# A conditioned attention block on one core: one order for the last slots, and k of tile 3, tile 4's division, tile 5's sums and x moved in the lead

## The chip, the core and the metric

The kernel runs on one NeuronCore of a Trainium2 chip. Its engines are TensorE (PE in the profile, matrix products), VectorE (DVE), ScalarE (ACT), GpSimd (POOL), and SyncE (SP), which issues most of the DMAs. They run side by side and wait for each other on semaphores only. Matrix products are written to PSUM banks (SA, SM, MB of two banks each, O and Y of one); everything else lies in SBUF. The metric is the device time of one execution in microseconds.

## What is computed

The reference, cut to what matters (16 batches of 512 tokens with 512 features; 16 heads of 32):

```
h = layernorm(x)                                   # over the features
shift, scale, gate = split(silu(time) @ mod_w + mod_b, 3)
h = h * (scale + 1) + shift
q, k, v = split_heads(h @ w_qkv)
q = rope(layernorm(q, q_norm_w), position)         # rotates the first 16 of 32 elements
k = rope(layernorm(k, k_norm_w), position)
attn = softmax(q @ k.T / sqrt(32))
out = x + (attn @ v) @ w_out * gate
```

## The kernel before, in words

Tokens are cut into 64 tiles of 128 (four a batch), heads into 64 groups of four (four a batch). Products that need precision are made in three passes, with a high part and a low part of each operand: `project` computes q, k or v of a tile with 12 matmuls of 512 columns, `project_out` the output of a tile with 12. `project_part` and `project_out(n, bank, first, last)` can run a piece of the twelve.

The order on each engine is written by hand. A lead fills the pipeline: weights are split in high and low parts, the first tiles normalized (`normalize_x`), moved, squared and summed (`square_sums`), divided by their roots (`inverse_roots`, `normalize_qk`), and rotated on GpSimd (`rotate`, three instructions for q and three for k). Then a loop of 64 slots, `for s in range(LAST + 1)`, where slot s does the attention of group s, the projections of tiles s + 4 to s + 6 and the output of tile s - 5:

- TensorE: `transpose_c(s)` (transposes the row maxima of group s), `transpose_qk(s + 1)`, then four times `scores_by_key(s, t)`, with `scores_by_query(s + 1, t)`, `weigh_values`, `add_over_keys(s - 1)`, projections and an output tile between them.
- VectorE takes the maxima of `scores_by_query` (`maxima`, two halves for each t), the low parts (`low_qk`, `x_low`), sums, roots and `apply_gate`.
- ScalarE takes the exponentials of `scores_by_key` (`key_exponentials`, two halves), and copies out of PSUM.
- GpSimd adds probs over keys: `add_keys` issues two DMAs of 1024 KB a group that add one buffer to another, `sum_keys` one addition of 2048 elements a partition; it also scales o (`scale_o`), makes its low part (`output_low`), adds the residual (`add_residual`), and rotates.

What binds them around the change: `scores_by_query(s + 1, t)` needs the first exponential of `scores_by_key(s, t)`, since both use bank SM; `scores_by_key(s, t + 1)` needs both exponentials of t and the first maximum of `scores_by_query(s + 1, t)`; `transpose_c(s + 1)` needs all eight maxima of its group. Bank Y is shared by projections, sums over keys and output tiles, one after the other.

Slots with `late(s)` (58 to 63) have no projections of q and k left. Before, slots 58 and 59 run the output tile between `scores_by_query(s + 1, 1)` and `scores_by_key(s, 2)`, slots 60 to 62 in two halves of six matmuls after the query scores of t = 0 and 1; slot 62 has one more behind its last query scores, and slot 63 one before `scores_by_key(63, 1)`. Behind the last query scores of slots 58 to 61 nothing stands.

## Time and profile before

| | |
|---|---|
| time, median of 3 runs | 1703.88 us (1703.47 to 1704.93) |
| profiled execution, own time | 1703.24 us |
| its span | 1701.0 us |
| TensorE busy | 1635.7 us (96%) |
| VectorE, ScalarE, GpSimd busy | 1238.0, 997.2, 977.0 us |
| mean granted clock | 0.987 |

The span is what the trace covers; what lies around it is 2.2 us. Times in the rows count from the start of the span. [...]

### The profile page before, as it was taken

The page shows a single profiled execution, that of the slowest core. Times are in us where ns is not written, and L with a number is a line of the kernel's source. Part 1 is how long each engine was busy: PE and PEld are TensorE (multiplying, and loading weights), DVE is VectorE, ACT ScalarE, POOL GpSimd, SP SyncE. Part 2 cuts the span into 40 slices and gives each one's busy share as a digit, 9 for nine tenths or more (in the row PEclk, how much of TensorE's full clock was granted, in tenths as well). Part 3 has the DMA queues.
Part 4 walks back from the last instruction along what each step waited for, and adds up shares of the span by engine and source line. Part 5 has one row for each costly group of instructions (what it writes and reads, how often), then busy time and mean ns, then how long its engine had stood idle before and what let it go on. Part 6 is the DMA issues. An engine that isn't in the chain of part 4 may idle for free.

```text
span 1701.0 us, 31069 instructions
## 1 busy us (share of the span) xinstructions
PE 1635.7 (96%) x11846; PEld 963.6 (57%) x11846; DVE 1238.0 (73%) x1541; ACT 997.2 (59%) x1484; POOL 977.0 (57%) x769
## 2 busy tenths in 40 slices
PE   5979999999999999999999999999999999999887
PEld 3744565556566556555656655655555665564444
DVE  8767777777777777777777777777777777776552
ACT  3445666656566566665656656666666665665552
POOL 0525556665656656666665665666666566565441
PEclk9979999999999999999999999999999999999999
DMA  6034545546455554644645555464555555545553
GB/s 218 26 69 87 122 109 134 128 106 149 112 118 131 121 134 106 151 110 111 144 112 130 119 137 118 107 149 112 125 131 119 122 120 137 116 109 117 128 112 96
DMA packets 55417, 204.25 MB, mean 120 GB/s; under 512 B 6872, under 2 KB 6872, under 8 KB 39144
## 3 DMA queue, kind: packets, MB, share of 16 engines
q0 software_dynamic: 18144, 132.13, 38.6%
q1 hardware_dynamic: 37128, 70.14, 12.8%
q8 instruction: 97, 1.59, 0.4%
q14 instruction: 48, 0.39, 0.1%
HBM read 53.25 MB, written 16.88 MB: 41 GB/s over the span
## 4 chain that ended last, share of the span: by engine, by line
PE 87%; DVE 3%; DMA 3%; issue 3%; POOL 2%; ACT 1%; SPq 0%; POOLq 0%; DVEq 0%; ACTq 0%
PE Y L339 33%; PE O L447 13%; PE SA L428 12%; PE Y L357 10%; PE SM L396 6%; PE MB L379 3%; PE SA L432 3%; PE Y L462 3%; DMA probs<-probs 2%; PE SA L331 2%; PE SA L406 1%; POOL probs L1287 1%; DMA probs<-in_L_cond_w_qkv_dram 1%; DVE cst L1053 1%; PE SM L428 0%
## 5 line engine op out<-in xcount | busy, mean ns | idle before, releaser
L1287 POOL TENSOR_TENSOR probs<-probs 128x2048 f32<-128x2048 f32 x62 | 285.5, 4605 | 334.0 <-DMA probs<-probs 334.0
L1053 DVE TENSOR_REDUCE cst<-SM 128x2 fp32r<-128x1024 f32 x256 | 313.8, 1226 | 141.1 <-PE MB L396 139.4
L808 ACT ACTIVATE probs<-SM 128x1024 f32<-128x1024 f32 x256 | 262.9, 1027 | 149.5 <-PE SM L432 140.5
L1053 DVE TENSOR_REDUCE cst<-MB 128x2 fp32r<-128x1024 f32 x256 | 311.3, 1216 | 0.0
L810 ACT ACTIVATE probs<-SA 128x1024 f32<-128x1024 f32 x256 | 260.6, 1018 | 0.0
L447 PE MATMUL O<-probs,vals 128*32 128x512 f32 x2048 | 250.8, 603 | 0.0
L339 PE MATMUL Y<-wqkv_hi,hT_lo 128*128 128x512 f32 x716 | 225.6, 411 | 0.4 <-DVE hT_lo L1037 0.4
L1260 POOL TENSOR_TENSOR pair_part<-rows,rope_pair 128x256 f32<-128x256 f32 x128 | 120.2, 939 | 171.0 <-DVE rows L1031 170.1
L339 PE MATMUL Y<-wqkv_hi,hT_hi 128*128 128x512 f32 x716 | 213.5, 420 | 0.0
L717 ACT ACTIVATE rows<-Y 128x512 f32<-128x512 f32 x121 | 72.3, 598 | 221.3 <-PE Y L339 221.3
L339 PE MATMUL Y<-wqkv_lo,hT_hi 128*128 128x512 f32 x716 | 201.5, 403 | 0.0
L1043 DVE SCALAR_TENSOR_TENSOR qk_lo<-MB,pass_w,qk_hi 128x512 fp32r<-128x512 f32 x128 | 90.7, 747 | 146.7 <-ACT qk_hi L753 146.3
L1279 POOL DMA_DIRECT2D probs<-probs x126 | 109.9, 872 | 139.0 <-PE O L447 134.1
L339 PEld LDWEIGHTS Y<-wqkv_lo,hT_hi 128*128 128x128 f32 x716 | 129.9, 188 | 75.3 <-issue 48.6
L339 PEld LDWEIGHTS Y<-wqkv_hi,hT_hi 128*128 128x128 f32 x716 | 120.6, 188 | 81.3 <-issue 23.2
L339 PEld LDWEIGHTS Y<-wqkv_hi,hT_lo 128*128 128x128 f32 x716 | 125.5, 188 | 51.1 <-issue 28.5
L396 PE MATMUL SM<-qk_hi 32*128 32x512 f32 x512 | 128.6, 498 | 15.8 <-ACT probs L808 11.0
L1066 DVE TENSOR_TENSOR gated<-Y,gate 128x512 f32<-128x512 f32 x60 | 41.5, 691 | 127.8 <-PE Y L357 127.8
L428 PE MATMUL SA<-qk_hi 32*128 32x512 f32 x512 | 128.8, 500 | 4.5 <-DVE cst L1053 3.8
L428 PE MATMUL SM<-qk_hi 32*128 32x512 f32 x512 | 129.0, 500 | 0.0
L396 PE MATMUL MB<-qk_hi 32*128 32x512 f32 x512 | 128.8, 498 | 0.0
L1293 POOL TENSOR_TENSOR oT<-oT,sum_inv 128x512 f32<-128x512 f32 x63 | 107.0, 1698 | 34.7 <-ACT sum_inv L781 34.7
(219 smaller groups left out, 3461.7 us busy)
## 6 DMA issues: line engine op xcount, KB each, us to landing
probs<-probs POOLq DMA_DIRECT2D x126, 1024.0 KB, 7.1
xin<-in_x_dram SPq DMA_DIRECT2D x62, 256.0 KB, 2.7
xres<-in_x_dram SPq DMA_DIRECT2D x60, 256.0 KB, 2.7
out_dram<-xres SPq DMA_DIRECT2D x60, 256.0 KB, 5.8
shift_scale<-mod_rows SPq DMA_DIRECT2D x15, 512.0 KB, 3.8
gate<-mod_rows SPq DMA_DIRECT2D x16, 256.0 KB, 3.3
rows<-in_L_cond_mod_w_dram SPq DMA_DIRECT2D x2, 1024.0 KB, 8.7
probs<-in_L_cond_w_qkv_dram SPq DMA_DIRECT2D x2, 1024.0 KB, 13.1
```

The costliest lines, as they stand in the source:

```text
L339: mm = pe.matmul(bank, x[:, k, :], w[:, k, cols], start=(m == 0), stop=(m == 3 * DT - 1))
L357: mm = pe.matmul(bank, o[:, g, :], w[:, g, :], start=(m == 0), stop=(m == 11))
L396: mm = pe.matmul(qm_bank(i), qk_hi[r, g % 2, 0, cols], qk_hi[r, g % 2, 1, :], start=True, stop=True)
L428: pe.matmul(s_bank(i), a[r, ring, 1, cols], c[r, ring, 0, :], start=(a is qk_hi and c is qk_hi), stop=False)
L447: mm = pe.matmul(O[head_rows(i), :], vals[:, b % 2, t, E * h:E * (h + 1)], probs[:, probs_buffer(g, t), i, :], start=(t == 0), stop=(t == ...
L808: act.activation(a[:, 2:4, :], SM[:], ACT.Exp).then_inc(s_exp, 1)
L810: act.activation(a[:, 0:2, :], SA[:], ACT.Exp).then_inc(s_exp, 1)
L1053: dve.tensor_reduce(heads[:, 2 * half:2 * half + 2, 0], (SM, MB)[half][:], AX.X, ALU.max, negate=True).then_inc(max_out, 1)
L1260: pool.tensor_tensor(pair_part[:].rearrange("p h (i two) -> p h i two", two=2), swapped, rope_pair[:, t, j, :].rearrange("p (i two) -> p i ...
L1279: pool.dma_start(probs[:, probs_buffer(g, t - 1)].rearrange("p h n -> p (h n)"), probs[:, probs_buffer(g, t)].rearrange("p h n -> p (h n)" ...
L1287: pool.tensor_tensor(total, total, part, ALU.add).then_inc(keys_summed, 1)
L1293: pool.tensor_tensor(o, o, sum_inv[:].rearrange("p (t n) -> p t n", t=TT), ALU.mult).then_inc(o_scaled, 1)
```

## The change

In the last slots, all output tiles come to stand behind the last query scores of a slot (slot 62 has a second one inside, slot 63's stands behind its third `scores_by_key`). `add_over_keys(62)` gets bank MB[1] in place of Y. `apply_gate`, `add_residual`, `output_high` and `output_low` of such a tile move to the start of the next slot. In the lead, VectorE rotates k of tile 3 (`rotate_k3`), `pass_weights` goes ahead, and on TensorE the order is another: v of tile 3 before x of tile 4 is transposed, group 0 transposed before x of tile 5, k of tile 4 cut around the first query scores, k of tile 5 in bank Y, v of tile 4 in slot 0. On VectorE, x of tile 6 goes behind the four pairs of maxima, and `square_sums(5, 0)` and `normalize_qk(4)` go into slot 0.

```diff
             def transpose_qk(g, j):
                 if i == 0:
-                    pe.wait_ge(rope_step, 6 * (TT * b + 3) + 3 * (j + 1))
+                    if b > 0:
+                        pe.wait_ge(rope_step, rope_steps(TT * b + 3, j) + 3)
+                    elif j == 0:
+                        pe.wait_ge(rope_step, rope_steps(3, 0) + 3)
+                    else:
+                        pe.wait_ge(k3_step, 3)
...
             project(2, 2, MB[:, 0, :])
-            transpose_x(4)
             pe.wait_ge(raw_out, raw_count(3, 1))
             project(3, 2, MB[:, 1, :])
+            transpose_x(4)
             modulation_parts(2, O[:])
...
@@ TensorE, the slots
-                if s > 0 and tile(s + 4):
+                if tile(s + 4):
                     if s > 1:
                         pe.wait_ge(sum_ln, s - 1)
                     if tile(s + 5):
                         pe.wait_ge(raw_out, raw_count(s + 5, 1))
+                    else:
+                        pe.wait_ge(y_gated, n)
...
-                elif group(s + 1) and n >= 0:
-                    pe.wait_ge(o_low, n + 1)
-                    pe.wait_ge(sum_ln, s - 1)
-                    project_out(n, Y[:], 0, 6)
...
                 if late(s):
                     weigh_values(s, 0)
                     if group(s + 1):
                         scores_by_query(s + 1, 1)
-                        if tile(s + 4):
-                            pe.wait_ge(o_low, n + 1)
-                            pe.wait_ge(v_out, s + 5)
-                            project_out(n, Y[:], 0, 12)
-                        else:
-                            project_out(n, Y[:], 6, 12)
...
+                    if s == LAST - 1:
+                        pe.wait_ge(o_low, n + 1)
+                        pe.wait_ge(y_gated, n)
+                        project_out(n, Y[:], 0, 12)
...
                         scores_by_query(s + 1, 3)
-                        if s == LAST - 1:
-                            pe.wait_ge(o_low, NT - TT - 1)
-                            pe.wait_ge(sum_ln, s)
-                            project_out(NT - TT - 2, Y[:], 0, 12)
+                        m = n + 1 if s == LAST - 1 else n
+                        pe.wait_ge(o_low, m + 1)
+                        pe.wait_ge(sum_ln, s)
+                        project_out(m, Y[:], 0, 12)
...
@@ VectorE
+            def rotate_k3():
+                dve.wait_ge(qk_norm, 4)
+                dve.wait_ge(silu_step, 2)
+                r = rows[:, 0, 3, 1, :].rearrange("p (h e) -> p h e", e=E)
+                part = oT_rows[:, 0, 0:H * R].rearrange("p (h r) -> p h r", r=R)
...
+                dve.tensor_tensor(part.rearrange("p h (i two) -> p h i two", two=2), swapped,
+                                  rope_pair[:, 3, 1, :].rearrange("p (i two) -> p i two", two=2)
+                                  .unsqueeze(1).to_broadcast([P, H, PAIRS, 2]), ALU.mult).then_inc(k3_step, 1)
+                dve.wait_ge(k3_step, 1)
+                dve.tensor_tensor(r[:, :, 0:R], r[:, :, 0:R], rope_same[:, 3, 1, :].unsqueeze(1)
+                                  .to_broadcast([P, H, R]), ALU.mult).then_inc(k3_step, 1)
+                dve.wait_ge(k3_step, 2)
+                dve.tensor_tensor(r[:, :, 0:R], r[:, :, 0:R], part, ALU.add).then_inc(k3_step, 1)
...
             for s in range(LAST + 1):
+                if late(s - 1):
+                    apply_gate(s - 6 if s < LAST else NT - TT - 2, Y[:], gated[:])
...
-                if s > 0 and tile(s + 5):
+                if tile(s + 5):
                     square_sums(s + 5, 0)
+                if s == 0:
+                    normalize_qk(4)
...
@@ GpSimd
                 rotate(n, 0)
-                rotate(n, 1)
+                if n != 3:
+                    rotate(n, 1)
...
+                if late(s - 1):
+                    add_residual(s - 6)
+                    output_low(s - 5)
                 if s > 0:
                     sum_keys(s - 1)
                 add_keys(s, 1)
-                if s - 5 >= 0 and not late(s):
+                if s - 5 >= 0 and not late(s) or s == LAST - 1:
                     add_residual(s - 5)
...
-                if late(s):
-                    add_residual(s - 5)
                 if s == LAST - 1:
                     output_low(s - 4)
                 add_keys(s, 3)
```

Three places in the order of the instructions. First TensorE at the end of slot 61, before: the value products of t = 2 (O), the last query scores (SM, MB), and then the transposition of the maxima (SA from cst) that opens the next slot.

```order
L447 MATMUL O<-probs,vals 32x512 x4
L396 MATMUL SM<-qk_hi 128x512 x2
L396 MATMUL MB<-qk_hi 128x512 x2
L406 MATMUL SA<-ident_r,cst 128x128 x4
L379 MATMUL MB<-ident,rows 128x128 x8
```

The same place with the change:

```order
L457 MATMUL O<-probs,vals 32x512 x4
L406 MATMUL SM<-qk_hi 128x512 x2
L406 MATMUL MB<-qk_hi 128x512 x2
L362 MATMUL Y<-wout_hi,o_hi 128x512
L362 MATMUL Y<-wout_lo,o_hi 128x512
L362 MATMUL Y<-wout_hi,o_lo 128x512
...
L416 MATMUL SA<-ident_r,cst 128x128 x4
L389 MATMUL MB<-ident,rows 128x128 x8
```

The twelve matmuls of an output tile (Y from wout and o) stand between the last query scores and the transposition.

Second, VectorE in the lead, before, from the division of tile 3 (rows from rstd) on: the low part of x of tile 4 (hT_lo), x of tile 5 (xin), the sum of the gate's parts (oT), the weights for the pass half, x_low of tile 5.

```order
L1031 TENSOR_TENSOR rows<-rows,rstd 128x1024
L1037 TENSOR_TENSOR hT_lo<-SA,hT_hi 128x512
L1021 SCALAR_TENSOR_TENSOR xin<-xin,first_stats,shift_scale 128x512
L1024 SCALAR_TENSOR_TENSOR xin<-xin,first_rstd,shift_scale 128x512
L948 TENSOR_TENSOR oT<-O,sum_inv 128x512
L1118 TENSOR_SCALAR pass_w<-pass_w 128x1
L1121 MEMSET pass_w 16x2 x4
L1037 TENSOR_TENSOR hT_lo<-SA,hT_hi 128x512
```

With the change:

```order
L1038 TENSOR_TENSOR rows<-rows,rstd 128x1024
L1061 TENSOR_TENSOR hT_lo<-SA,hT_hi 128x512
L1049 TENSOR_TENSOR oT<-rows,rope_pair 128x256
L1053 TENSOR_TENSOR rows<-rows,rope_same 128x16x16
L1056 TENSOR_TENSOR rows<-rows,oT 128x16x16
L1028 SCALAR_TENSOR_TENSOR xin<-xin,first_stats,shift_scale 128x512
L1031 SCALAR_TENSOR_TENSOR xin<-xin,first_rstd,shift_scale 128x512
L955 TENSOR_TENSOR oT<-O,sum_inv 128x512
L1067 SCALAR_TENSOR_TENSOR qk_lo<-MB,pass_w,qk_hi 128x512 x2
```

Three instructions of the rotation stand before x of tile 5, and the low parts of q and k (qk_lo) follow at once.

Third, GpSimd in slot 62, before: the sums over keys (probs), the first DMA, scale_o (oT from sum_inv), the residual, the low part of o.

```order
L1287 TENSOR_TENSOR probs<-probs 128x2048
L1279 DMA probs<-probs 128x2048
L1293 TENSOR_TENSOR oT<-oT,sum_inv 128x4x128
L1273 TENSOR_TENSOR xres<-xres,gated 128x512
L1298 TENSOR_TENSOR o_lo<-oT,o_hi 128x512
L1279 DMA probs<-probs 128x2048
```

With the change:

```order
L1299 TENSOR_TENSOR xres<-xres,gated 128x512
L1324 TENSOR_TENSOR o_lo<-oT,o_hi 128x512
L1313 TENSOR_TENSOR probs<-probs 128x2048
L1305 DMA probs<-probs 128x2048
L1299 TENSOR_TENSOR xres<-xres,gated 128x512
L1319 TENSOR_TENSOR oT<-oT,sum_inv 128x4x128
L1324 TENSOR_TENSOR o_lo<-oT,o_hi 128x512
L1305 DMA probs<-probs 128x2048
```

The residual and the low part of tile 56 and 57 open the slot, and the residual of tile 57 stands ahead of scale_o.

## Rows read from the trace of the kernel before

**Rows 1.** The page: granted clock of TensorE in 40 slices, in tenths

```profile
PEclk9979999999999999999999999999999999999999
```

**Rows 2.** Windows: stretch, length, busy of five engines, clock, DMA; slots 1, 58 to 63

```profile
122.17:146.10 23.93, 22.16 (x172) 12.26 (x171) 17.39 (x22) 14.87 (x22) 12.50 (x10) 1.00 0.48 100
1544.90:1566.54 21.64, 18.07 (x149) 9.74 (x148) 14.52 (x18) 13.79 (x20) 12.81 (x11) 1.00 0.49 99
1566.54:1590.61 24.07, 20.46 (x156) 10.95 (x157) 11.62 (x11) 12.46 (x16) 11.56 (x9) 0.93 0.55 120
1590.61:1612.12 21.51, 17.72 (x144) 8.75 (x145) 11.53 (x11) 11.97 (x15) 10.80 (x7) 0.91 0.66 141
1612.12:1634.67 22.55, 19.00 (x145) 9.24 (x145) 11.52 (x11) 12.01 (x15) 10.13 (x7) 0.86 0.55 117
1634.67:1659.69 25.02, 22.07 (x157) 11.95 (x157) 11.52 (x11) 11.74 (x15) 10.18 (x7) 0.86 0.60 127
1659.69:1701.00 41.31, 31.28 (x217) 17.47 (x215) 12.46 (x17) 11.70 (x15) 7.56 (x6) 0.95 0.31 93
```

**Rows 3.** Waits of TensorE, 1546 to 1701: us in total, times, longest

```profile
PE SA L406 <- DVE cst L1053: 9.8, 4, 2.5
PE Y L357 <- POOL o_lo L1298: 5.3, 2, 3.5
```

**Rows 4.** Timeline of slot 60: start, us, engine, line, operation, idle before and releaser

```profile
1602.40 0.50 PE L428 MATMUL SM<-qk_hi 32*128 32x512 f32 x2
...
1606.75 0.50 PE L428 MATMUL SM<-qk_hi 32*128 32x512 f32 x2
...
1609.15 0.50 PE L396 MATMUL SM<-qk_hi 32*128 32x512 f32 x2 [0.21 <-ACT probs L808]
...
1612.12 0.75 PE L406 MATMUL SA<-ident_r,cst 128*128 128x128 f32 x4 [2.46 <-DVE cst L1053]
```

**Rows 5.** Timeline of slot 58's start, and two matmuls of an output tile

```profile
1544.90 0.46 PE L406 MATMUL SA<-ident_r,cst 128*128 128x128 f32 x4
...
1546.24 0.50 PE L428 MATMUL SM<-qk_hi 32*128 32x512 f32 x2
...
1550.99 0.50 PE L428 MATMUL SM<-qk_hi 32*128 32x512 f32 x2
...
1580.09 0.39 PE L357 MATMUL Y<-wout_hi,o_hi 128*128 128x512 f32 x1
1580.32 0.39 PE L357 MATMUL Y<-wout_lo,o_hi 128*128 128x512 f32 x1
```

**Rows 6.** Timeline of slots 62 and 63: residual adds and waits for o_lo

```profile
1655.25 0.50 PE L357 MATMUL Y<-wout_hi,o_hi 128*128 128x512 f32 x1 [1.79 <-POOL o_lo L1298]
...
1664.03 1.26 POOL L1273 TENSOR_TENSOR xres<-xres,gated 128x512 f32<-128x512 f32 x1 [8.04 <-DMA xres<-in_x_dram]
...
1666.57 0.80 PE L357 MATMUL Y<-wout_hi,o_hi 128*128 128x512 f32 x1 [3.52 <-POOL o_lo L1298]
```

**Rows 7.** TensorE in the lead: a wait of 60 to 122, and the timeline

```profile
PE SM L396 <- DVE cst L1053: 4.8, 2, 4.5
...
95.62 0.72 PE L406 MATMUL SA<-ident_r,cst 128*128 128x128 f32 x4 [2.51 <-issue]
```

**Rows 8.** Timeline: GpSimd beside VectorE in slot 56, and wout_lo in the lead

```profile
1514.00 1.80 POOL L1293 TENSOR_TENSOR oT<-oT,sum_inv 128x512 f32<-128x512 f32 x1
...
1514.68 1.67 DVE L1024 SCALAR_TENSOR_TENSOR xin<-xin,rstd,shift_scale 128x512 f32<-128x512 f32 x1
...
75.00 4.58 POOL L1304 TENSOR_TENSOR wout_lo<-probs,wout_hi 128x2048 fp32r<-128x2048 f32 x1
```

**Rows 9.** VectorE's groups by form, 60 to 125: busy, mean ns, idle before

```profile
L1053 DVE TENSOR_REDUCE cst<-SM 128x2 fp32r<-128x1024 f32 x8 | 9.8, 1223 | 8.4 <-PE MB L396 8.4
L1031 DVE TENSOR_TENSOR rows<-rows,rstd 128x1024 f32<-128x1024 f32 x4 | 4.9, 1226 | 0.1
```

**Rows 10.** Windows: a stretch of slot 0, columns as in rows 2

```profile
105.00:110.00 5.00, 3.67 (x24) 1.49 (x24) 2.65 (x4) 2.98 (x5) 0.00 (x0) 0.51 0.07 25
```

More of the change, by code:

```diff
@@ L461, in add_over_keys @@
                     for i in range(HG):
-                        mm = pe.matmul(Y[head_rows(i), :], ones_r[:, 0:E].bitcast(F32),
+                        mm = pe.matmul(bank[head_rows(i), :], ones_r[:, 0:E].bitcast(F32),
                                        probs[:, probs_buffer(g, t), i, :],
@@ L528, in _ @@
             project(4, 0, Y[:])
-            transpose_x(5)
-            project(4, 1, SA[:, 0, :])
             transpose_qk(0, 0)
@@ L562, in _ @@
                         pe.wait_ge(raw_out, raw_count(s + 5, 1))
-                begun = 5 if s > 0 and not late(s - 1) else 0
+                    else:
+                        pe.wait_ge(y_gated, n)
+                begun = 5 if not late(s - 1) else 0
                 if begun:
@@ L567, in _ @@
                     scores_by_query(s + 1, 0)
-                if s > 0 and tile(s + 4):
+                if tile(s + 4):
                     project_part(s + 4, 2, Y[:], begun, 12)
-                elif group(s + 1) and n >= 0:
-                    pe.wait_ge(o_low, n + 1)
-                    pe.wait_ge(sum_ln, s - 1)
-                    project_out(n, Y[:], 0, 6)
-                if s == LAST:
-                    pe.wait_ge(o_low, NT - TT)
-                    pe.wait_ge(y_gated, NT - TT - 1)
-                    project_out(NT - TT - 1, Y[:], 0, 12)
                 scores_by_key(s, 1)
@@ L613, in _ @@
                             pe.wait_ge(v_out, s + 5)
-                        add_over_keys(s - 1)
+                        add_over_keys(s - 1, Y[:])
                 scores_by_key(s, 2)
                 if late(s):
-                    weigh_values(s, 1)
                     if group(s + 1):
+                        weigh_values(s, 1)
                         scores_by_query(s + 1, 2)
-                        pe.wait_ge(y_gated, n + 1)
-                        add_over_keys(s - 1)
-                    else:
+                        if tile(s + 4):
+                            pe.wait_ge(v_out, s + 5)
+                        pe.wait_ge(y_gated, n + 1 if s == LAST - 1 else n)
+                        add_over_keys(s - 1, Y[:])
+                    else:
+                        pe.wait_ge(o_low, NT - TT)
+                        pe.wait_ge(y_gated, NT - TT - 1)
+                        project_out(NT - TT - 1, Y[:], 0, 12)
+                        weigh_values(s, 1)
                         add_last_sums(1)
-                        pe.wait_ge(last_low, 2)
-                        project_last(0, 0, 2)
                 else:
@@ L649, in _ @@
                         pe.wait_ge(sum_ln, LAST)
+                        pe.wait_ge(last_low, 2)
+                        project_last(0, 0, 2)
+                        pe.wait_ge(y_gated, NT - TT)
                         project_last(1, 0, 2)
@@ L854, in _ @@
             move_v(2, MB[:, 0, :])
-            x_high(4)
             guess_roots(5)
             move_v(3, MB[:, 1, :])
+            x_high(4)
             move_qk(4, 0, Y[:])
-            x_high(5)
-            square(4, 0)
-            move_qk(4, 1, SA[:, 0, :])
             high_qk(0, 0)
             high_qk(0, 1)
+            square(4, 0)
             act.wait_ge(mod_product, 3)
             act.activation(mod_sb[:, 2, :], O[0:NB, :], ACT.Copy).then_inc(gate_out, 1)
+            x_high(5)
+            move_qk(4, 1, SA[:, 0, :])
             square(4, 1)
@@ L880, in _ @@
                 key_exponentials(s, 0, 0)
+                if late(s - 1) and s < LAST:
+                    output_high(s - 5)
                 key_exponentials(s, 0, 1)
@@ L887, in _ @@
                     square(s + 5, 1)
-                if s > 0 and tile(s + 4):
+                if tile(s + 4):
                     move_v(s + 4, Y[:])
@@ L912, in _ @@
                 key_exponentials(s, 3, 1)
-                if 0 <= s - 4 and s < LAST - 1:
+                if 0 <= s - 4 and not late(s):
                     output_high(s - 4)
@@ L1152, in _ @@
             first_statistics(2)
+            pass_weights()
             square_sums(2, 0)
@@ L1163, in _ @@
             x_low(4)
+            rotate_k3()
             normalize_x(5)
             modulation_sum(2, 2, O[:])
-            pass_weights()
+            low_qk(0, 0)
+            low_qk(0, 1)
             x_low(5)
@@ L1190, in _ @@
                     low_qk(s + 1, 1)
-                if s > 0 and tile(s + 5):
+                if tile(s + 5):
                     square_sums(s + 5, 0)
+                if s == 0:
+                    normalize_qk(4)
                 if group(s + 1):
@@ L1210, in _ @@
                     maximum(s + 1, 1, 1)
-                if late(s) and s < LAST:
+                if s == LAST - 1:
                     apply_gate(s - 5, Y[:], gated[:])
@@ L1330, in _ @@
                 add_keys(s, 3)
-                if 0 <= s - 4 and s < LAST - 1:
+                if 0 <= s - 4 and not late(s):
                     output_low(s - 4)
```

44 lines of the change are left out of this document (21 added, 23 removed).

## The prediction

> **What bounds the kernel now.** I read the page's clock line first. [...] TensorE is busy 1635.7 of 1701.0 us, so in the 57 slots in the middle only less matmul work would help, and the change leaves these slots as they are. It can win only where TensorE idles: in the lead (before slot 0 and in it) and in slots 58 to 63. So I read the tail slot by slot, then who TensorE waited for there, then the timeline.
>
> A slot here runs from one transposition of the row maxima (transpose_c) to the next. Slots 58 to 63 take 21.64, 24.07, 21.51, 22.55, 25.02 and 41.31 us, 156.1 in all, and from slot 59 on the granted clock is below 1 [rows 2]. The waits name two causes: 9.8 us in 4 waits for VectorE's maxima, and 5.3 us in 2 waits for GpSimd's o_lo [rows 3]. The timeline shows the first: key products start at 1602.40 and 1606.75, the last query scores at 1609.15, and then nothing until transpose_c at 1612.12, 2.46 us idle. [...] The second cause is 1.79 us idle at 1655.25 and 3.52 us at 1666.57, the latter because GpSimd had waited for a residual's load until 1664.03 [rows 6].
>
> In the lead, two waits for maxima of group 0 cost 4.8 us and one more, put down to nothing, 2.5 us; transpose_c of slot 0 starts at 95.62 [rows 7], that of slot 1 at 122.17. Slot 0 is thus 26.55 us long, against 23.93 for slot 1 [rows 2], though slot 0 has no v projection and no sums over keys.
>
> **The tail.** Nothing is removed from TensorE; the twelve matmuls of an output tile (halves of six in slots 60 and 61, a full run inside slots 58 and 59) now stand behind the last query scores. One such matmul starts 0.23 us after the other [rows 5], so the run is 12 x 0.23 = 2.75 us. It covers the 2.46 us idle: the same engine does this work while VectorE takes its two maxima. What it leaves behind is the inner intervals. An interval from key product to key product is 4.35 us [rows 4], set by a ring (exponential, query scores, first maximum), not by TensorE's work: the half runs hid inside it and it does not shrink. So the slots become:
> - transpose_c to first key product 1.34, and 4.75 us to the next where a v projection is split [rows 5]; 4.45 without filler and 5.7 where the whole run of 2.75 stands (estimates: 2.5 us until the query scores, 0.43 of them, then the maximum or the run);
> - 4.35 for each other interval; last interval 2.43 + 0.43 + 2.75 = 5.6, say 5.7;
> - slot 58: 1.34 + 4.75 + 4.35 + 4.35 + 5.7 = 20.5. Slot 59: with 5.7 in the place of 4.75, 21.4. Slots 60 and 61: with 4.45, 20.2 each.
> - Slot 62: a run in its second interval, 5.65; its last run waits for o_lo, which comes 1.26 us earlier since the residual add that stood before it moves ahead of scale_o [rows 6]. Of 1.79 us idle 0.5 stays. 1.34 + 4.45 + 5.65 + 4.35 + 6.3 = 22.1.
> - Slot 63: the run for tile 59 moves behind the third key product, where o_lo has been ready for 3 us, so the 3.52 goes. The clock of 0.95 over 41.31 us [rows 2] means 4.1 us at half clock, 2.1 of loss, which goes with the idles. In their place TensorE now waits openly for the first two exponentials: 1.0 to 1.3. 41.31 - 3.5 - 2.1 + 1.3 = 37.0, say 37.2.
>
> The sum is 141.6 against 156.1: **14.5 us less** if the clock holds. What may not hold is the clock. Seven inner intervals have now only key product, one weighing and query scores, and idle about 0.2 and 1.4 us. The nearest rows are on both sides: slot 1 idles 1.2 and 0.4 us around its second query scores and is granted 1.00 [rows 2], while every 2.46 us [rows 3] was followed by a fall. One fall costs about 1.1 us in a ring (key product 0.7, query scores 0.3). From none to five is 0 to 5.5 us. I take one, nearer to slot 1: **tail -13.3**.
>
> GpSimd's queue in a late slot becomes residual, o_lo, sum_keys, then the DMA that adds probs. The DMA of the last keys goes out about 0.25 us earlier and took some 8 us to land, so it is there 4.3 us after the next first key product; exponentials want it at 5.7. No new wait, 1.4 us to spare. SP's stores and loads of residuals start earlier relative to the end, which is what frees tile 58's.
>
> **The lead.** On VectorE k of tile 3 is three instructions of 256 elements. No row has them; a 1024-element one takes 1.23 and a 512-element one 0.69, so 0.41 each, 1.2 us, up to twice that beside GpSimd. GpSimd loses three of 0.74. So both rotations end some 2 us earlier than before, but wout_lo, one instruction of 4.58 us [rows 8], starts earlier too: at about 71.3, exactly when VectorE comes to normalize_x(5), two instructions whose inputs all lie in SBUF. [Rows 8] show what such a meeting does: scale_o, at best 1.27 us, took 1.80, since VectorE was at the first x instruction; the second x instruction then took 1.67 in place of 0.74, until GpSimd was done. Before, nothing of the kind stood beside wout_lo. So I let VectorE stand still until it ends, 75.7.
>
> [...]
>
> With the wait: x 5 is ready at 77.2, modulation_sum(2) at 77.9 (plus 0.5 since pass_weights now delays VectorE at 57), and TensorE has stood for 5 us before the gate's product. Product, copy, transposition, x_high, x_low, square sums, statistics: 5.7, to 84.1. Four pairs of maxima at 2 x 1.2 us each [rows 9], with division and square sums between and one wait for k of tile 5: 12.2, to 96.3. So transpose_c of slot 0 comes **0.7 later** than before. Slot 0 then takes what slot 1 takes, 23.93, less the 0.9 of the sums over keys, plus 0.6 of cold start: 23.6. v of tile 4, twelve matmuls, hides in intervals that idle now; the division of tile 4 delays the first maximum by 0.5, counted. Slot 1 starts at 119.9 in place of 122.17: **lead -2.2**.
>
> Sum: -13.3 - 2.2 = -15.5. The profiled execution took 1703.24 (span 1701.0 plus 2.2); the median of the runs is 1703.88, so 1703.88 - 15.5 = **1688.4 us**.
>
> **Rivals.**
> - No block in the lead. The 4.6 us instruction may give way piecemeal, or VectorE may pass before it. Then everything up to slot 1 is 4.3 us earlier: 1684. For it: no row has a block that long. Against: both meetings in [rows 8] lasted to the other's end.
> - The lean intervals lose the clock again and again: five falls in place of one, and part of the same in slot 0. 1688.4 + 4.4 + 1.5 = 1694.
> - Slower than before: the clock doesn't come back in the late slots. In slot 0 it stays at 0.51 over 105 to 110 though TensorE is busy for 3.67 of 5 us [rows 10], with gaps before the query scores and behind them, just the pattern that the change makes. If this lasts through slots 58 to 62, their 15 us of work a slot become about 28, 8 us over the interval ring's 20.2: 5 x 8 = 40 in place of a gain of 13, so 1703.9 - 2.2 - 13.3 - 1.2 + 40 = 1727. It decides from the point where two of five late slots stay at half clock throughout. Against: each slot ends in 5 us with hardly a gap, after which the rows show full clock.
> - The change does nothing in the tail, since another wait takes its place (the exponentials' wait for the DMA in slot 63, or y_gated before the sums over keys): 1701 to 1702.
>
> [...]
>
> **The numbers.** Forecast 57%, no block 22%, clock lost repeatedly 14%, no gain 3%, stuck clock 3%, 1% for the lead going wrong by itself. The range 1681.5 to 1696 takes in the first three: below it stands -6.5 in the lead with -14.5 and 1 us to spare, above it five falls and a lead that gains nothing. A difference under 0.2% (3.4 us) can hardly be told from none: faster by more 0.95, within 0.02, slower by more 0.03.
>
> **What would show it.** TensorE's waits for VectorE's maxima in the tail fall from 9.8 us to under 1, and the runs of an output tile end right before transpose_c; o_lo is waited for 0.5 us. Slots 60 and 61 are 20.2 us with clock above 0.93. In the lead normalize_x(5) shows one instruction of about 5 us beside wout_lo, and transpose_c of slot 1 stands near 119.9. I am wrong in the tail if these slots stay above 21.5 us, and in the lead if no such instruction is there.

## The result, and the profile after

The changed kernel takes **1695.78 us** (median of 6 executions, 1694.55 to 1698.43) against 1704.51 for the kernel before (6 executions, 1703.47 to 1704.93). The ratio is 0.9952, with a 95% interval of 0.9939 to 0.9965: faster by 8.2 us by the ratio and by 8.7 by the medians, where 15.5 were forecast. The time lies just inside the range, the sign is right, the size is not.

The profiled execution took 1696.27 us, its span 1694.3. This is its clock line (page of the changed kernel), the counterpart of [rows 1]:

```profile
PEclk9999999999999999999999999999999999999899
```

The dip near the start is gone from this line, and one near the end has come. The clock is a share of full clock. Over 70 to 130 us, in windows of 0.5 us, it reads 1.00 or 0.50, and something between only where it changes (0.50 from 99 to 102, 1.00 from 103 to 108): 0.50 is called the lower level, or half clock, here. To see where the time went I cut the trace at transpose_c of each slot (now L416), as in [rows 2]. Windows of the changed kernel: stretch, length, busy time of TensorE, its weight loads, VectorE, ScalarE and GpSimd, granted clock, DMA. The first row is slot 0, the others slots 58 to 63:

```profile
97.60:123.83 26.23, 24.59 (x164) 13.48 (x165) 19.66 (x25) 12.81 (x18) 10.71 (x14) 0.87 0.29 71
1546.92:1567.70 20.78, 17.99 (x149) 9.95 (x148) 14.20 (x17) 13.27 (x19) 12.70 (x11) 1.00 0.51 103
1567.70:1590.25 22.55, 20.21 (x157) 10.39 (x156) 11.53 (x11) 12.46 (x16) 10.15 (x6) 0.92 0.55 120
1590.25:1613.29 23.04, 19.71 (x145) 8.77 (x144) 11.54 (x11) 11.73 (x15) 10.06 (x6) 0.78 0.57 123
1613.29:1634.21 20.92, 17.38 (x145) 8.29 (x144) 11.53 (x11) 11.80 (x15) 9.99 (x6) 0.92 0.63 139
1634.21:1656.38 22.17, 18.83 (x157) 10.23 (x156) 12.23 (x12) 12.26 (x16) 12.53 (x8) 1.00 0.68 163
1656.38:1694.20 37.82, 29.90 (x217) 16.43 (x215) 13.41 (x17) 11.70 (x15) 7.73 (x6) 0.98 0.32 94
```

The span became 6.7 us shorter, and it splits like this:

| stretch | before | after | difference | forecast |
|---|---|---|---|---|
| start to transpose_c of slot 0 | 95.62 | 97.60 | +1.98 | +0.7 |
| slot 0 | 26.55 | 26.23 | -0.32 | -2.9 |
| slots 1 to 57 | 1422.73 | 1423.09 | +0.36 | 0 |
| slots 58 to 63 | 156.10 | 147.38 | -8.72 | -13.3 |

So the tail gives two thirds of what it should, and the lead, which should give 2.2, takes 1.7. Within the tail, slots 58 and 62 are as forecast (20.5 and 22.1). Slots 59, 60 and 61 (forecast 21.4, 20.2, 20.2) hold 4.7 us of the miss, and these three have a clock of 0.92, 0.78 and 0.92.

Waits of TensorE from 1530 to 1695 (who waited, for whom: us in all, times, longest), to be read against [rows 3]:

```profile
PE SA L438 <- DVE cst L1077: 11.0, 10, 1.4
PE SM L406 <- ACT probs L815: 3.7, 15, 0.5
...
PE Y L362 <- POOL o_lo L1324: 0.6, 1, 0.6
PE MB L472 <- DMA probs<-probs: 0.5, 1, 0.5
```

The four waits of 2.5 us ahead of transpose_c are gone and so are the long waits for o_lo, as forecast. But VectorE's maxima are still waited for, by the key products now, 11.0 us in ten pieces of up to 1.4: the idle has moved into the slots.

Timeline of slot 60, two intervals from key product to key product in which only one weighing and the query scores stand (start, us, engine, line, operation, idle before and its releaser):

```profile
1593.97 0.49 PE L406 MATMUL SM<-qk_hi 32*128 32x512 f32 x2 [0.23 <-ACT probs L815]
...
1595.89 0.50 PE L438 MATMUL SA<-qk_hi 32*128 32x512 f32 x2 [1.42 <-DVE cst L1077]
...
1597.03 1.89 PE L457 MATMUL O<-probs,vals 128*32 128x512 f32 x8
1598.85 0.79 PE L406 MATMUL SM<-qk_hi 32*128 32x512 f32 x2
...
1601.07 0.79 PE L438 MATMUL SA<-qk_hi 32*128 32x512 f32 x2 [1.43 <-DVE cst L1077]
```

After the idles of 0.23 and 1.42 us the weighing takes 1.89 us (1.07 in the interval before) and a pair of query scores 0.79 (0.49): the clock is at its lower level (0.50 from 1597.1 to 1607.4). It stays there for two intervals. In slot 58 the same two idles stand in the second interval (0.23 at 1555.43 and 1.42 at 1557.36), and the weighing behind them took 1.07 us: there the clock did not fall (1.00 over the slot). In slot 59 they stand in the second interval too (1.42 at 1579.16), and the weighing behind took 1.94: there it fell (0.50 from 1580.6 to 1582.6).

The lead: rows of all engines around wout_lo, and the two places further on where TensorE stood:

```profile
71.82 0.85 DVE L1056 TENSOR_TENSOR rows<-rows,oT 128x256 f32<-128x256 f32 x1
72.34 4.69 POOL L1330 TENSOR_TENSOR wout_lo<-probs,wout_hi 128x2048 fp32r<-128x2048 f32 x1
...
72.59 4.99 DVE L1028 SCALAR_TENSOR_TENSOR xin<-xin,first_stats,shift_scale 128x512 f32<-128x512 f32 x1
...
77.62 0.75 DVE L1031 SCALAR_TENSOR_TENSOR xin<-xin,first_rstd,shift_scale 128x512 f32<-128x512 f32 x1
...
79.03 1.89 PE L542 MATMUL O<-oT,gated 128*16 128x512 f32 x2 [5.50 <-DVE oT L955]
...
97.60 0.51 PE L416 MATMUL SA<-ident_r,cst 128*128 128x128 f32 x4 [2.51 <-issue]
```

The block is there as forecast: an instruction that takes 0.74 us without wout_lo beside it (experiment 3) lasted 4.99, until wout_lo was done (77.03), and TensorE stood for 5.50 us. No semaphore stands between the two instructions, so it isn't true of this pair that the engines wait for each other on semaphores only.

### The profile page after: what moved, and what is told of

The parts are those of the page before. It is cut to its first block, busy times and chain, and to the rows that moved or that the text cites. A ratio compares the mean times of both kernels' runs of the same rounds, so it can differ in the third digit from the quotient of the medians.

```text
span 1694.3 us, 31069 instructions
## 1 busy us (share of the span) xinstructions
PE 1633.5 (96%) x11846; PEld 959.8 (57%) x11846; DVE 1244.3 (73%) x1544; ACT 996.9 (59%) x1484; POOL 973.3 (57%) x766
## 3 DMA queue, kind: packets, MB, share of 16 engines
q0 software_dynamic: 18144, 132.13, 38.6%
q1 hardware_dynamic: 37128, 70.14, 12.9%
## 4 chain that ended last, share of the span: by engine, by line
PE 91%; DVE 4%; DMA 2%; issue 1%; ACT 1%; POOL 0%; SPq 0%; DVEq 0%; POOLq 0%; ACTq 0%
PE Y L344 33%; PE O L457 13%; PE SA L438 13%; PE Y L362 10%; PE SM L406 6%; PE SA L442 3%; PE MB L389 3%; PE Y L472 3%; PE SA L336 2%; DMA probs<-probs 1%; PE SA L416 1%; DVE cst L1077 1%; ACT probs L815 1%; DMA probs<-in_L_cond_w_qkv_dram 1%; PE SM L438 0%
## 5 line engine op out<-in xcount | busy, mean ns | idle before, releaser
L344 PEld LDWEIGHTS Y<-wqkv_lo,hT_hi 128*128 128x128 f32 x720 | 130.7, 188 | 75.5 <-issue 48.6
L1090 DVE TENSOR_TENSOR gated<-Y,gate 128x512 f32<-128x512 f32 x60 | 41.5, 692 | 128.4 <-PE Y L362 128.4
```

The source lines that it names most:

```text
L344: mm = pe.matmul(bank, x[:, k, :], w[:, k, cols], start=(m == 0), stop=(m == 3 * DT - 1))
```

## The experiments

Every kernel was timed side by side with the kernel before (1704.1 to 1704.5); times are medians, and ratios are to the kernel before beside it, with 95% intervals.

**1 and 2: the two halves of the change by themselves.** tail_only is the changed kernel with the lead, and the v projection of slot 0, as before. lead_only is the kernel before with the other part.

> Only the tail's part of the change; the lead and slot 0 are those of the kernel before. Theory A (the trace of the changed kernel is right that its lead loses 1.7 us and its slots 58 to 63 gain 8.7): the tail alone gains 8.7 us, 1704.5 - 8.7 = 1695.8, some 2 us LESS than or level with the whole change plus what its lead loses: whole change 1695.8, tail alone 1694.1. Rival B (the lead helps as predicted, and the tail gives the rest): tail alone 1698, slower than the whole change by 2. Slots 58 to 63 in the trace: 147.4 us in all, as in the changed kernel, with one to four falls of the granted clock in slots 59 to 61.

> Only the lead's part of the change; the tail is that of the kernel before. Theory A: the lead by itself costs 1.7 us, 1706.2, with transpose_c of slot 0 at 97.6 and of slot 1 at 123.8. Rival B (as predicted, the trace of the one profiled execution being untypical): it gains 2.2 us, 1702.3, with transpose_c of slot 1 near 120.

| | time | ratio | interval |
|---|---|---|---|
| tail_only | 1695.27 | 0.9946 | 0.9934 to 0.9959 |
| lead_only | 1706.06 | 1.0013 | 1.0004 to 1.0021 |

Theory A holds in the gain that it gives for the tail alone (8.7, 1695.8); its other number, 1694.1, does not come out. The tail gives 8.9 us, and the lead costs about 2 (transpose_c of slot 1 at 124.90 in lead_only). The two ratios multiplied give 0.9959, within the interval of the whole change. The whole was no slower than the tail alone by more than the measurement tells (expected 1.7, found 0.5).

**3: wout_lo later.** One wait more on GpSimd:

```diff
                     pool.wait_ge(wout_high, 1)
+                    pool.wait_ge(h_lo, 6)
                     pool.tensor_tensor(wout_lo[:], wout_raw, wout_hi[:].bitcast(F32), ALU.subtract
```

> The changed kernel, with one more wait ahead of GpSimd's wout_lo: it starts only when the low part of x of tile 5 is written (h_lo 6), so that no VectorE instruction with two SBUF inputs meets it before that. Theory A (VectorE stands still behind wout_lo for its whole 4.7 us, and this is on the path to slot 0): the first x instruction of tile 5 takes 0.8 instead of 4.99 us, the gate's product on TensorE starts near 75 instead of 79.0, and transpose_c of slot 0 near 93.5 instead of 97.6; slot 1 begins 3 to 4 us earlier, 1692 us in all. Rival C (the block is hidden: another chain, as GpSimd's q rotation or the high parts of k, would set the time anyway): transpose_c of slot 0 moves by less than 1 us and the time is that of the changed kernel.

Measured: 1688.90 us, ratio 0.9908 (0.9892 to 0.9923). Rows of late_wout: x of tile 5, wout_lo, transpose_c of slot 0, and the window of slot 0:

```profile
72.79 0.74 DVE L1028 SCALAR_TENSOR_TENSOR xin<-xin,first_stats,shift_scale 128x512 f32<-128x512 f32 x1
...
78.09 4.56 POOL L1331 TENSOR_TENSOR wout_lo<-probs,wout_hi 128x2048 fp32r<-128x2048 f32 x1 [5.51 <-DVE hT_lo L1061]
...
93.80 0.72 PE L416 MATMUL SA<-ident_r,cst 128*128 128x128 f32 x4 [2.51 <-issue]
```

```profile
93.80:121.37 27.57, 25.93 (x164) 14.79 (x165) 19.67 (x25) 13.00 (x18) 10.71 (x14) 0.82 0.28 68
```

The x instruction is back at 0.74 us, and transpose_c of slot 0 comes 3.8 us earlier. Rival C falls. The median gained 6.9, 3.1 more than that, and this trace can't show it all, since the profiled execution was the slowest of this kernel's four (1693.72; the fastest 1686.57): its slot 0 is 1.3 us longer than that of the changed kernel, at a clock of 0.82. A part it does show. Behind a wait of 1.62 us for maxima at 81.65, eight matmuls of the lead took 1.84 and 1.91 us for four (the clock is 0.50 from 83.5 to 86). In the trace of combo (experiment 6), whose lead is the same, they took 1.08 and 1.07 (1.00 from 82 to 86), and transpose_c of slot 0 came at 91.88. So the block cost 3.8 us with a fall of the clock in the lead, and 5.7 without.

**4: wout_lo in four pieces** of 512 columns, at its old place in the queue.

```diff
-                    pool.tensor_tensor(wout_lo[:], wout_raw, wout_hi[:].bitcast(F32), ALU.subtract
-                                       ).then_inc(wout_low, 1)
+                    for c in range(DT):
+                        pool.tensor_tensor(wout_lo[:, c, :], wout_raw[:, c, :], wout_hi[:, c, :].bitcast(F32),
+                                           ALU.subtract).then_inc(wout_low, 1)
```

> The changed kernel with wout_lo made by four GpSimd instructions of 512 columns in place of one of 2048, at the same place in the queue. Theory A1 (a VectorE instruction with two SBUF inputs waits for the end of the one GpSimd instruction that runs, no longer): the first x instruction of tile 5 takes at most 1.2 + 0.8 = 2 us in place of 4.99, and the second perhaps as long again; x of tile 5 is ready 2 to 3 us earlier than 78.37, and the kernel takes 1692 to 1693. Rival A2 (GpSimd keeps its hold from one instruction to the next, or the contention is by the byte and not by the instruction): the two x instructions together still take 4.5 to 5.7 us, and the time stays at 1695.8.

Measured: 1692.23 us, ratio 0.9928 (0.9916 to 0.9940). The timeline of quarters, GpSimd and VectorE:

```profile
72.42 6.03 POOL L1331 TENSOR_TENSOR wout_lo<-probs,wout_hi 128x512 fp32r<-128x512 f32 x4
...
72.66 1.76 DVE L1028 SCALAR_TENSOR_TENSOR xin<-xin,first_stats,shift_scale 128x512 f32<-128x512 f32 x1
74.45 1.64 DVE L1031 SCALAR_TENSOR_TENSOR xin<-xin,first_rstd,shift_scale 128x512 f32<-128x512 f32 x1
```

The two engines take turns: each x instruction waits for one piece and then runs, 3.4 us together in place of 5.74, and the four pieces take 6.03 in place of 4.69. So in these two traces the wait goes by the instruction that is running (Theory A1), not by the bytes: 4.99 us beside one instruction of 4.69, and 1.76 beside a piece of 512 columns, which took 1.28 to 1.71.

The same trace has a slot 0 that the others without fillers have not:

```profile
94.01:117.20 23.19, 21.53 (x165) 12.49 (x165) 19.85 (x25) 12.79 (x18) 11.39 (x14) 1.00 0.34 81
```

Its order of matmuls is that of the changed kernel, and so are its idles (2.51 us ahead of transpose_c, 1.22 and 0.41 in the second interval), yet the clock held 1.00, and the slot took 23.19 us in place of 26.23. This was one of the two fastest of six executions (1688.93; 1688.81 to 1694.89).

**5: fillers in the tail.** Matmuls whose result nobody reads, where TensorE idles 1.42 us:

```diff
+            def fill(count):
+                for _ in range(count):
+                    pe.matmul(Y[:], ident_r[:], wout_hi[:, 0, :], start=True, stop=True)
...
                     project_part(s + 4, 2, Y[:], begun, 12)
+                elif group(s + 1):
+                    pe.wait_ge(y_gated, n)
+                    fill(4)
...
                         scores_by_query(s + 1, 1)
+                        if s < LAST - 1:
+                            if tile(s + 4):
+                                pe.wait_ge(v_out, s + 5)
+                            else:
+                                pe.wait_ge(y_gated, n)
+                            fill(4)
```

> The changed kernel, with four more matmuls (128 x 512, identity times the first rows of wout_hi, into bank Y, whose content nobody reads then) behind the query scores of every lean interval: the second interval of slots 58 to 61 and the first of slots 60 to 62, 28 matmuls of 0.23 us in all. They fit into the 1.42 us that TensorE idles there. Theory D (slots 59 to 61 are 4.6 us longer than forecast because the granted clock falls in lean intervals, the ring itself being as forecast): no fall in slots 59 to 61, these slots 21.4, 20.2 and 20.2 us instead of 22.55, 23.04 and 20.92, 4 us less, 1692 in all, and the runs spread less than the 3.9 us of the changed kernel. Rival E (the slots are longer for another cause, such as VectorE, the exponentials or a DMA): no gain, and if the fillers delay the key products, 0.2 us more for each of seven intervals, 1697.

Measured: 1692.89 us (1691.19 to 1693.39), ratio 0.9933 (0.9920 to 0.9945). Windows of fill_tail, slots 59, 60 and 61:

```profile
1568.99:1590.51 21.52, 19.90 (x161) 10.88 (x160) 11.53 (x11) 12.45 (x16) 10.16 (x6) 1.00 0.57 125
1590.51:1610.61 20.10, 18.22 (x154) 9.49 (x153) 11.53 (x11) 11.86 (x15) 10.13 (x6) 1.00 0.66 141
1610.61:1630.65 20.04, 18.15 (x154) 9.47 (x153) 11.53 (x11) 11.86 (x15) 10.03 (x6) 1.00 0.66 145
```

Theory D: with eight more matmuls in slots 60 and 61 and four in slot 59, each of the three is shorter, by 1.03, 2.94 and 0.88 us, and within 0.2 of the forecast. I see nothing but the clock (1.00 now) behind it, since the fillers add work and remove no wait. Slots 58 and 62, at 1.00 already in the changed kernel, got four fillers each too and did not become shorter (20.84 and 22.23 us against 20.78 and 22.17). The median gained 2.9 and the spread fell from 3.9 to 2.2 us. The trace's gain in the three slots is 4.85; of it slot 0, which these fillers don't touch, took 1.1 back (27.36 us, clock 0.83), and slot 63 became longer (38.6 against 37.9), in it a wait of 1.1 us for the DMA that adds probs (0.5 in the changed kernel).

**6: both repairs** (late wout_lo and the tail's fillers).

> The changed kernel with both repairs: wout_lo waits for the low part of x of tile 5, and the fillers in the lean intervals. Theory: the two act at different places, 1500 us apart, so their gains add up: -6.9 (late wout_lo as measured) and -2.9 (fillers as measured) from 1695.8, 1686 us. Rival: the gains overlap, since a part of the first was luck with the granted clock in the tail; then 1689, the time of the late wout_lo alone.

Measured: 1685.49 us (1685.12 to 1690.30), ratio 0.9897 (0.9884 to 0.9909). The gains add up.

**7: fillers in the lead as well.**

```diff
             pe.wait_ge(ident_ready, 1)
+            pe.wait_ge(wout_high, 1)
+            pe.wait_ge(gate_out, 1)
+            fill_o(9)
...
                     else:
+                        if s > 0:
+                            pe.wait_ge(o_out, s)
+                        fill_o(4)
                         scores_by_query(s + 1, 1)
                         transpose_x(s + 6)
```

> The kernel with both repairs, and fillers also at the start: nine matmuls of 0.23 us into bank O while TensorE waits 2.51 us for the last maxima of group 0, and four ahead of the second query scores in slots 0 to 4, where it waits 1.23 us for exponentials. Theory F (slot 0 is 26.2 to 27.6 us long, in place of the forecast 23.6, because the granted clock is 0.5 in its first 4 us and again after the idle of its second interval): full clock throughout slot 0 and a slot 0 of 24 to 24.5 us, 3 us less than without, 1683 in all. Rival G (the ring of exponentials and maxima sets slot 0, TensorE's clock only hides in it): slot 0 changes by less than 1 us.

Measured: **1683.35 us** (1682.09 to 1683.73), ratio 0.9875 (0.9861 to 0.9889), the best of all. Windows of combo_lead, slot 0 and slot 58:

```profile
93.75:116.97 23.22, 22.72 (x168) 13.18 (x169) 19.90 (x25) 12.78 (x18) 11.41 (x14) 1.00 0.33 81
1539.91:1560.43 20.52, 19.13 (x154) 10.64 (x152) 13.82 (x17) 13.27 (x19) 12.80 (x11) 1.00 0.51 103
```

Slot 0 is 23.22 us with the clock at 1.00, against the forecast 23.6 and 26.23 to 27.57 in the traces of this lead at 0.82 to 0.87. Theory F holds. Against combo, the kernel that differs by these fillers alone, the median is 2.1 us lower; combo's profiled execution had a slot 0 of 24.58 at 0.93, and that of quarters 23.19 at 1.00, so the clock isn't lost as much in every execution.

**8: the lead's fillers alone** in the changed kernel.

> The changed kernel with the lead's fillers alone: nine matmuls of 0.23 us before transpose_c of slot 0, four ahead of the second query scores in slots 0 to 4; wout_lo stays where the change puts it. Theory F (half clock in slot 0 costs 3 us of its forecast): transpose_c of slot 0 still at 97.6 (the block stays), slot 0 23.2 us in place of 26.2, slots 58 to 63 as in the changed kernel; 1695.8 - 3 = 1692.8. Rival G: slot 0 within 1 us of 26.2.

Measured: 1692.57 us, ratio 0.9925 (0.9911 to 0.9938). Window of slot 0 of lead_fill:

```profile
97.69:120.89 23.20, 22.69 (x168) 13.21 (x169) 19.88 (x25) 12.79 (x18) 11.41 (x14) 1.00 0.33 81
```

transpose_c of slot 0 stays at 97.69, since the block is still there, and slot 0 is 3.0 us shorter. The two causes in the lead are separate: the block before slot 0, the clock in it. The tail's code is that of the changed kernel, but the falls lie elsewhere in this trace: slots 59 to 62 take 22.33, 21.02, 21.86 and 23.46 us, at 0.92, 0.92, 0.84 and 0.93.

**9: k of tile 3 rotated by GpSimd again**, in the kernel of experiment 7 (rotate_k3 taken out, `rotate(3, 1)` put back).

> The kernel with all repairs (late wout_lo, fillers in the tail and in the lead), but k of tile 3 is rotated by GpSimd again, behind q. GpSimd's three instructions of 0.74 us put the end of k at about 74.6 instead of 72.7; VectorE in turn has 2.3 us less to do and comes to x of tile 5 at 70.4 instead of 72.8. Theory K (once wout_lo is out of the way, both chains meet at the gate's product near 75, so it matters little who rotates): 1683.4 within 1 us. Rival L (the rotation on VectorE is what brings the lead forward): transpose_c of slot 0 comes 2 us later, at 95.7, 1685.3.

Measured: 1685.19 us, ratio 0.9888 (0.9875 to 0.9902). In its trace k of tile 3 is ready at 75.5 and TensorE waits for it for 1.8 us, and transpose_c of slot 0 stands at 94.06, only 0.3 later than in combo_lead. But the two traces differ in the clock too: eight matmuls of combo_lead's lead took 1.81 and 1.91 us for four, those of k3_back 1.08 and 1.07. Against combo, whose lead has rotate_k3 and no such fall (91.88), k3_back is 2.2 us later, which is rival L's 2. The time, 1.8 us above experiment 7, is also nearer to rival L (1685.3) than to Theory K (1683.4 within 1). Yet the two kernels were not timed side by side and the intervals of their ratios overlap, so rival L is favoured and not shown.

**10 and 11: the kernel before, with fillers.** before_fill has ten behind the last query scores of slots 58 to 61, where it idles 2.46 us [rows 4]; before_fills has those of the lead too.

> The kernel before, with ten matmuls of 0.23 us (into bank Y, read by nobody) behind the last query scores of slots 58 to 61, where it idles 2.46 us. They hold the granted clock and take away no wait. Theory H (the idle itself cost 2.46 a slot, and the fall of the clock behind it about 1.1 to 1.5 more): transpose_c stays where it was relative to the last maxima, slots 59 to 62 lose only the falls, 4 us in all, 1700.3. Rival I (the half clock behind each idle is hidden by the ring of maxima, so that only the idle counted): no gain, 1704.

> The kernel before with all fillers (ten behind the last query scores of slots 58 to 61, nine before transpose_c of slot 0, four in slots 0 to 4) and its own order. It shows how much of the gain is the clock's alone. Theory: 4.4 us from the tail's fillers as measured and 3 from slot 0 (26.6 to 27.5 us long, with half clock inside; 23.5 to 24 with it held), 1704.3 - 7.4 = 1697; the kernel with all repairs is then 13.6 us faster by its order alone. Rival: slot 0 of the kernel before is bound by its ring and gains under 1 us, 1699.5.

| | time | ratio | interval |
|---|---|---|---|
| before_fill | 1700.05 | 0.9975 | 0.9965 to 0.9985 |
| before_fills | 1695.83 | 0.9953 | 0.9941 to 0.9966 |

Windows of before_fill, slots 59 to 63:

```profile
1567.19:1590.00 22.81, 21.44 (x168) 11.88 (x167) 11.53 (x11) 12.35 (x16) 11.65 (x9) 1.00 0.58 127
1590.00:1609.97 19.97, 18.63 (x155) 9.61 (x155) 11.43 (x11) 11.74 (x15) 10.81 (x7) 1.00 0.69 152
1609.97:1631.44 21.47, 18.69 (x156) 9.64 (x155) 11.44 (x11) 11.75 (x15) 10.08 (x7) 1.00 0.58 123
1631.44:1653.67 22.23, 19.06 (x157) 10.14 (x157) 11.43 (x11) 11.63 (x15) 10.22 (x7) 1.00 0.62 131
1653.67:1697.30 43.63, 32.15 (x217) 17.98 (x215) 12.45 (x17) 11.70 (x15) 7.55 (x6) 0.89 0.32 94
```

Slots 59 to 62 became 6.7 us shorter against [rows 2], by the clock alone; slot 63 gave 2.3 back, in its trace a wait of 5.1 us for o_lo in place of 3.5. Theory H. Holding the clock in the old order (before_fills, 1695.83) is worth as much as the whole change (1695.78). The new order with the clock held and the block out of the way is 12.5 us better than that.

The traces with fillers also tell what the order by itself is worth in each slot. From the old order to the new, with the clock at 1.00 in both, slot 58 went from 21.65 to 20.52 us, slot 59 from 22.76 to 21.51, slot 60 from 19.98 to 20.04, slot 61 from 20.15 to 20.05 (before_fills and combo_lead), and slot 62 from 22.23 (before_fill) to 22.24. Slot 63 went from 41.5 to 37.4, with a part for the clock: over its first 37 us it was 0.95 and 0.99, by estimate 1.5 us of the 4.1. In slots 60, 61 and 62 the order by itself gained nothing; where the kernels differ there, it is by the clock.

## Why the prediction was right or wrong

**The lengths of the tail's slots were right, for a clock that holds.** The run of an output tile covers the 2.46 us ahead of transpose_c: no wait is left at a slot's end. o_lo was waited for 0.6 us (forecast 0.5). With the clock held, slots 58 to 62 take 20.84, 21.52, 20.10, 20.04 and 22.23 us in fill_tail against 20.5, 21.4, 20.2, 20.2 and 22.1 forecast: the sum of this step was good to 0.4 us. What the account missed is where the gain came from. In slots 60 and 61 the idle moved into the intervals, and the old order with the clock held is as short (19.98 and 20.15); the new order by itself gains 1.1 and 1.3 us in slots 58 and 59 and about 2.6 in slot 63. The rest of the 14.5 is the price of the old falls, which comes only as far as the new order has none. One sign that I had named contradicts my own sum: waits for maxima under 1 us, where seven intervals with 1.4 us idle make 10. They are 11.0.

**The step that failed in the tail: "I take one" fall of the clock.** The price of a fall was right (forecast 1.1 us; 1.03 in slot 59, 0.88 in slot 61), and slot 60, which stayed at the lower level for some 10 us, lost 2.94. Together 4.85 us, nearly the 5.5 of the five falls in my second rival, to which I gave 14%. (Slot 60: a clock of 0.78 over 23.04 us is 2 x 0.22 x 23.04 = 10.1 us at half clock.) I had taken slot 1, with its idles of 1.2 and 0.4 us at 1.00 [rows 2], as the nearest row, and as if its 1.00 belonged to the pattern. It belonged to that execution. Slot 1's order is the same in all kernels here. Its value products behind the two idles took 1.92 us in five of the nine traces without fillers in slot 1, among them that of the kernel before and that of the changed kernel, and 3.00 to 3.25 in the other four. The timeline of late_wout:

```profile
129.89 0.50 PE L406 MATMUL SM<-qk_hi 32*128 32x512 f32 x2 [1.22 <-ACT probs L815]
...
131.66 3.25 PE L457 MATMUL O<-probs,vals 128*32 128x512 f32 x16
```

With the lead's fillers, which fill the first of the two idles, they took 1.92 in four traces of four. Slots 58 and 59 of the changed kernel say the same: one pattern, one fall in two. So do the traces of one tail: slot 61 held 1.00 in late_wout and quarters and fell in the changed kernel, slot 62 the other way round (23.48 and 23.49 us against 22.17). A pattern of this kind falls in some slots and some executions and not in others, and the change makes more of them: seven intervals with 0.2 and 1.4 us idle in place of four with 2.46.

Slots 59 to 61 of the changed kernel, at 0.92, 0.78 and 0.92, and slot 1 of late_wout, at 0.93, have the lower level behind idles of 0.2 to 1.4 us; slot 1 at 1.00 in one trace was no evidence against that.

**Slot 63** took 37.9 (forecast 37.2). The 4.1 us at half clock that I reckoned with there, and the 2.1 of loss, rest on a lower level of 0.50, which the trace before shows (0.50 from 98 to 99 us). The 3.52 us wait went, the open wait for exponentials is 1.0. The DMA that adds the last probs landed 10.6 us after its issue, where I had taken some 8 and 1.4 us to spare: ScalarE waited 2.6 us for it, and TensorE 0.5. Over the traces of kernels with the new tail the slot is between 37.2 and 38.6 us long.

**The lead: the mechanism was right, its start was not.** VectorE stood behind wout_lo to its end, as the forecast had it and the first rival had not. But VectorE and GpSimd rotated at the same time, and the rotation on VectorE took 0.57, 0.84 and 0.85 us, 2.3 in place of 1.2 (I had said "up to twice that" and then reckoned with once). wout_lo started at 72.34 instead of 71.3, took 4.69 for 4.58, and a slip of 0.2 stands in the sum besides (71.3 and 4.58 are 75.9, not 75.7): the block ended at 77.03. Of the 1.0, 0.4 are the later division of tile 3, which I had booked behind the block as 0.5 for pass_weights. So the gate's product came 0.6 later than forecast (79.03 for 78.4), and the four pairs of maxima took 12.9 for 12.2. Together that is the 1.3 by which transpose_c of slot 0 came later than forecast. Behind its wait of 5.50 us TensorE ran at half clock besides (0.50 from 80 to 84).

**The step that failed in the lead: slot 0 at 23.6.** It took 26.23. Windows of the changed kernel in and before slot 0:

```profile
76.00:80.00 4.00, 0.97 (x2) 0.13 (x2) 3.96 (x5) 0.00 (x0) 1.03 (x1) 0.78 0.00 0
80.00:84.00 4.00, 4.00 (x14) 2.20 (x12) 1.66 (x4) 1.18 (x2) 0.00 (x0) 0.50 0.27 77
...
96.00:100.00 4.00, 2.40 (x20) 2.01 (x24) 3.55 (x5) 1.79 (x3) 0.00 (x0) 0.84 0.00 0
100.00:104.00 4.00, 4.00 (x24) 2.35 (x21) 3.01 (x5) 2.46 (x3) 1.35 (x2) 0.74 0.00 0
...
108.00:112.00 4.00, 3.59 (x24) 1.02 (x20) 3.27 (x6) 1.42 (x4) 0.24 (x1) 0.62 0.24 70
```

I allowed 0.6 us for a cold start, an estimate that no run shows. In its place the clock fell twice, behind the 2.51 us ahead of transpose_c (0.50 from 99 to 102) and behind the idles of the second interval (0.50 from 109 to 112), and the fillers show the price: 26.23 to 23.20. Neither fall is certain: quarters, with these idles and no fillers, had 23.19. I had also measured slot 1 badly: its stretch in [rows 2] ends at 146.10, while the next transpose_c stands at 146.48, so slot 1 is 24.3 us long. With 24.3 in place of 23.93, and without the 0.6 for a cold start, the sum for an undisturbed slot 0 is 23.4; the forecast of 23.6 was 0.4 above the 23.2 measured, and near it because the two slips partly cancel. And the gain of 2.9 that I booked for it wasn't the order's at all: slot 0 of the kernel before, with fillers, is 23.30 us long. v of tile 4 does hide in idle time, so it costs nothing, but it brings nothing to slot 0 either.

**Slower, or nothing in the tail.** The rival of a stuck clock (1727) had something right, the long stay at the lower level in slot 60, but it ended there: the twelve matmuls at the slot's end were again at full clock (1.00 from 1610.5 on).

**In sum**, 9.0 us are missing from the span by the unrounded terms (8.8 by the rounded sum): 3.6 in slots 59 to 61 beyond the one fall allowed, 1.1 in slots 58, 62 and 63, 2.6 in slot 0, 1.3 ahead of it, and 0.4 in slots 1 to 57, where nothing was changed. Slots 59 to 61 and slot 0, which are 6.2 of it, are settled by the fillers. Slots 1 to 57 differ between traces: 1423.8 to 1424.1 us in the four that fell in slot 1, and 1422.7 to 1423.2 in all others, that of the changed kernel (1423.1) among them.

## What to carry to other kernels

When a long idle is filled by taking filler out of several short ones, count what the short ones become, and how many follow each other: here 4.9 us, a third of the 14.5 that the tail was to give with the clock held, went to a clock that fell in intervals that idled 1.65 of 4.35 us, and that had shown 1.00 over such a pattern in the one trace I had. Before the order gets the credit for a slot that became shorter, run the old order with the clock held as well: in slots 60 to 62 it was as short. Four matmuls into a bank that nobody reads, put where the engine waits anyway, show in one run how much of a slot's length is the clock, and they may stay. When an instruction is moved in a queue, ask what it then stands beside. Here the long GpSimd instruction did no harm where VectorE took maxima out of PSUM (1.19 and 1.22 us beside wout_lo in late_wout, 1.22 behind it), and less in pieces (3.4 us for the two x instructions in place of 5.74).

## What the runs showed of the hardware

- The first x instruction of VectorE, with its inputs in SBUF (0.74 us in late_wout, where GpSimd waits), stood for 4.99 us beside one GpSimd instruction of 4.69, and for 1.76 beside a piece of it with a quarter of the columns; in quarters the two x instructions, 1.76 and 1.64 us, each stood beside a piece of its own.
- Idles of 0.23 and 1.42 us, with matmuls between them and all around, were followed by the lower level of the clock (0.50) in slots 59, 60 and 61 and not in slot 58 of one execution. With 0.9 us of the 1.42 filled, the clock was 1.00 in all of these slots.
- The same lead ran at half clock behind a wait of 1.6 us in late_wout (0.50 from 83.5 to 86, four matmuls in 1.84 and 1.91 us) and not in combo (1.00, 1.08 and 1.07); the same slot 0 took 26.23 us at 0.87 in one trace and 23.19 at 1.00 in another.
- The executions of the changed kernel spread by 3.9 us, with mean clocks from 0.987 to 0.992, and the slowest has the lowest clock. With all fillers they spread by 1.6 us, at 0.997 to 0.998. The falls account for the spread, as far as these few runs can tell.
- The fillers cost more in a lead whose clock was already low. In before_fills the nine at the lead's end stood at a clock of 0.50 and took 4.21 us (2.32 in combo_lead, at 1.00), longer than the 2.51 us wait that they stand in, and transpose_c of slot 0 came at 97.34 instead of 95.62:

```profile
92.60 0.79 PE L396 MATMUL SM<-qk_hi 32*128 32x512 f32 x2 [4.50 <-DVE cst L1070]
...
93.33 4.21 PE L481 MATMUL O<-wout_hi,ident_r 128*128 128x512 f32 x9
97.34 0.67 PE L406 MATMUL SA<-ident_r,cst 128*128 128x128 f32 x4
```
